# One third of the routed rows formed by GpSimd, the rest by ScalarE one behind each product

## What is computed

```python
mu = jnp.mean(xf, axis=-1, keepdims=True)
var = jnp.var(xf, axis=-1, keepdims=True)
...
tk_probs, tk_idx = jax.lax.top_k(probs, TOP_K)
...
out = _swiglu(xf, sWg, sWu, sWd)
for e in range(NUM_EXPERTS):
    out = out + w[:, e:e + 1] * _swiglu(xf, Wg[e], Wu[e], Wd[e])
return out.reshape(B, S, H)
```

## Time and profile before

| | us |
|---|---|
| median of 3 runs | 2165.62 (2164.62 to 2167.09) |
| the profiled execution | 2157.81, its span 2156.2 |
| granted TensorE clock, mean | 0.978 |
| busy: PE, DVE, ACT, POOL | 1972.2, 1245.1, 1079.3, 800.1 |
| front stage in the trace | about 1173 to 1490 |

### The profile page before, as it was taken

How to read it: one execution, slowest core, us unless ns; L and a number is a source line. 1 busy time by engine, 2 the same in 40 slices (tenths; PEclk the granted TensorE clock), 3 DMA queues, 4 the chain that set the end, 5 groups by cost and what they waited for, 6 DMA issues and landing times. The chain is left out here.

```text
span 2156.2 us, 48396 instructions
## 1 busy us (share of the span) xinstructions
PE 1972.2 (91%) x14823; PEld 1296.1 (60%) x14824; DVE 1245.1 (58%) x3875; ACT 1079.3 (50%) x2352; POOL 800.1 (37%) x1164
## 2 busy tenths in 40 slices
PE   2689999999999999999988999997999999999997
PEld 1344444454444554445545887785777777777776
DVE  5656667766667666676653954443545554545454
ACT  1245555555555555555543454452555555555553
POOL 3023323333323333233332046661444444444443
PEclk8789999999999999999989999998999999999999
DMA  7234443344443434434313355553873333333332
GB/s 239 70 93 116 120 130 117 120 116 120 136 131 111 127 109 127 131 114 132 106 63 114 110 166 207 200 185 117 221 181 58 57 53 55 55 59 55 54 55 36
DMA packets 156640, 246.08 MB, mean 114 GB/s; under 512 B 29408, under 2 KB 90592, under 8 KB 156480
## 3 DMA queue, kind: packets, MB, share of 16 engines
q1 hardware_dynamic: 120960, 189.24, 28.6%
q0 software_dynamic: 32064, 53.44, 12.0%
q10 hardware_dynamic: 3456, 1.34, 0.3%
HBM read 111.89 MB, written 90.50 MB: 94 GB/s over the span
## 5 line engine op out<-in xcount | busy, mean ns | idle before, releaser
L680 DVE CUSTOM_DVE_ANT_0 ps_rows<-ps_rows,maskrow 128x128 f32<-128x128 f32 (+1 forms) x1009 | 477.3, 514 | 295.5 <-PE ps_rows L525 287.6
L623 ACT ACTIVATE probs<-ps_cols 128x512 f32<-128x512 f32 (+3 forms) x1024 | 391.9, 435 | 391.8 <-PE ps_cols L536 385.1
L525 PE MATMUL ps_rows<-ks,qs 32*128 32x512 f32 x1984 | 406.8, 484 | 72.9 <-DVE mx L680 36.0
L532 PE MATMUL ps_cols<-qs,ks 32*128 32x512 f32 (+3 forms) x2048 | 421.9, 488 | 2.3 <-ACT probs L623 2.2
L1624 POOL DMA_INDIRECT out_dram<-y_e,to x135 | 215.5, 1596 | 348.9 <-DMA out_dram<-y_e,to 229.3
L799 POOL TENSOR_TENSOR pace<-eps 1x1 f32<-1x1 f32 x256 | 58.0, 227 | 752.6 <-ACT probs L623 752.6
L525 PEld LDWEIGHTS ps_rows<-ks,qs 32*128 32x128 f32 x1984 | 154.2, 185 | 270.0 <-DVE mx L680 223.3
L536 PE MATMUL ps_cols<-mT,ones_r 32*128 32x512 f32 (+3 forms) x1024 | 287.1, 554 | 0.0
L1753 DVE TENSOR_TENSOR h_lo<-ps_h,h_hi 128x512 fp32r<-128x512 f32 x135 | 93.4, 692 | 232.8 <-ACT h_hi L1728 232.8
L1722 ACT ACTIVATE sg_e<-ps_ge 128x512 f32<-128x512 f32 x135 | 80.8, 598 | 261.7 <-PE ps_ge L1646 261.7
L554 PE MATMUL ps_o<-probs,vt 128*32 128x512 f32 (+3 forms) x2048 | 193.7, 451 | 0.8 <-POOL probs L801 0.8
(11 more groups left out here) (218 smaller groups left out, 3852.0 us busy)
## 6 DMA issues: line engine op xcount, KB each, us to landing
xs_d<-zrows SPq DMA_DIRECT2D x45, 408.0 KB, 2.9
xr<-xs_d POOLq DMA_DIRECT2D x135, 136.0 KB
whi_d<-w_sh SPq DMA_DIRECT2D x16, 768.0 KB, 3.8
w_hi<-whi_d SPq DMA_DIRECT2D x24, 512.0 KB
xn<-in_L_attn_x_dram SPq DMA_DIRECT2D x16, 512.0 KB, 5.3
ks<-k_lin SPq DMA_DIRECT2D x64, 128.0 KB, 2.7
ks<-k_tan SPq DMA_DIRECT2D x64, 128.0 KB, 3.7
qs<-q_lin SPq DMA_DIRECT2D x64, 128.0 KB, 2.4
```

The source lines that it names most:

```text
L525: mm = nc.tensor.matmul(ps_rows[bank_of(row_no(g, it, h))][:, 0:(it + 1) * P], qs[at:at + STRIP, d.par, g, it * P:(it + 1) * P], ks[at:at ...
L532: nc.tensor.matmul(ps_cols[bank_of(col_no(n, s, e))][:, jt * P:S], ks[at:at + STRIP, b.par, gc, jt * P:(jt + 1) * P], qs[at:at + STRIP, b. ...
L623: nc.scalar.activation(probs[:, n % 2, 2 * (1 - s) + e, jt * P:S], ps_cols[bank_of(col_no(n, s, e))][:, jt * P:S], ACT.Exp).then_inc(exp_d ...
L680: nc.vector.tensor_tensor_reduce(out=bank, in0=bank, in1=maskrow[:, (TT - 1 - it) * P:S], scale=1.0, scalar=LOWEST, op0=ALU.add, op1=ALU.m ...
```

## The change

Every third tile, `own(t)`: t % 3 == 2, 21 of the 64, is formed by GpSimd itself, in its loop right before that tile's scatters, with a `tensor_scalar` (times `rstd2`, plus `nmr`) and a `tensor_copy` of `place`. They count a new semaphore, `pool_normed`. ScalarE forms the other 43, one a call: four a batch, still from batch 4 on; tile 63 stays in slot 2 of batch 14. Before each pair of scatters GpSimd waits for both counts, and SyncE does before it reloads an `xw` buffer; when it tries to is as before (six tiles a batch).

```diff
-    A_ROUND = (2, 1, 2, 1)
...
+    def own(t):
+
+        return t % 3 == 2
+
+    ACT_TILES = [t for t in range(NT) if not own(t)]
+
     def tiles_of(s, i):
 
-        n = sum(A_ROUND)
-        first = (s.off - ROWS_AT) * n + sum(A_ROUND[:i])
-        many = A_ROUND[i] if s.off < FIRST - 1 else 2
-        return range(max(first, 0), min(first + many, NT)) if s.off >= ROWS_AT else range(0)
+        at = (s.off - ROWS_AT) * IT + i
+        return ACT_TILES[at:at + 1] if s.off >= ROWS_AT else []
+
+    def formed(t):
+
+        return 2 * sum(1 for u in range(t + 1) if not own(u)), 2 * sum(1 for u in range(t + 1) if own(u))
...
             if bt >= AHEAD:
-                sp.wait_ge(normed, (bt - AHEAD + 1) * TT * 2)
+                by_act, by_pool = formed((bt - AHEAD + 1) * TT - 1)
+                sp.wait_ge(normed, by_act)
+                sp.wait_ge(pool_normed, by_pool)
...
         for t in range(NT):
             q = t % RING
-            pool.wait_ge(normed, (t + 1) * 2)
+            if own(t):
+                bt = t // TT
+                pool.wait_ge(xw_loaded[bt % AHEAD], (bt // AHEAD + 1) * 16)
+                if t >= RING:
+                    pool.wait_ge(scattered[q], t // RING * 32)
+                nc.gpsimd.tensor_scalar(row[q][:, :, 0:D], xw[:, bt % AHEAD, t % TT].unsqueeze(1).to_broadcast([P, 2, D]),
+                                        rstd2[:, t:t + 1], nmr[:, t:t + 1], ALU.mult, ALU.add).then_inc(pool_normed, 1)
+                nc.gpsimd.tensor_copy(row[q][:, :, D:D + 2], place[:, t]).then_inc(pool_normed, 1)
+            pool.wait_ge(normed, formed(t)[0])
+            pool.wait_ge(pool_normed, formed(t)[1])
```

More of the change, by code:

```diff
@@ L1255, in front_stage @@
     normed = sem("normed")
+    pool_normed = sem("pool_normed")
     scattered = [sem(f"scattered{q}") for q in range(RING)]
@@ L1303, in _ @@
                 se.load_in(sp, Batch(0, s + 2))
-            while loaded < NB and (loaded - AHEAD + 1) * TT <= (s - ROWS_AT) * sum(A_ROUND):
+            while loaded < NB and (loaded - AHEAD + 1) * TT <= (s - ROWS_AT) * 6:
                 load_rows(loaded)
@@ L1348, in norm_rows @@
                 bt, q = t // TT, t % RING
-                if t % TT == 0:
-                    act.wait_ge(xw_loaded[bt % AHEAD], (bt // AHEAD + 1) * 16)
+                act.wait_ge(xw_loaded[bt % AHEAD], (bt // AHEAD + 1) * 16)
                 if t == 0:
```

## The result

| | before | after |
|---|---|---|
| median, us | 2166.36 (2164.62 to 2167.80, 4 runs) | 2137.78 (2137.74 to 2140.31, 4 runs) |
| ratio | | 0.9873, 95% interval 0.9858 to 0.9888 |
| profiled execution, its span | 2157.81, 2156.2 | 2137.79, 2136.1 |

The change makes the kernel 28.6 us (1.3%) faster.

What follows compares the result with a forecast made beforehand. The prediction took a loop through GpSimd's scatters, not TensorE's floor, as the bound. Forming 44.0 plus usual gaps 3.0 minus filled gaps 39.0 gave +8.0 us on 2165.6, so 2174 (chance 0.38), range 2149 to 2188.

Steps and rivals of the forecast that it cites:

- What bounds the kernel: Front stage: completions visible only after GpSimd's scatter run pauses, so a GpSimd loop of 19.5 us paces, not TensorE's 17.55.
- Relief of ScalarE 0: Front stage: taking 21 us of tile forming from ScalarE gains 0, as its wait for TensorE hides that work.
- pairs 0: ScalarE's forming of tiles in pairs in slots 0 and 2 by itself costs TensorE nothing.
- SyncE 0: Before reloading xw, SyncE also waits for GpSimd's tiles: 0 unless GpSimd is a whole round behind.
- end 0: End of front stage: 23 us of TensorE's work follow tile 63 before and after, so the loop's loss carries through in full.
- A tile costs 2.2 us: GpSimd's forming: TENSOR_SCALAR 1.6, COPY 0.2, completion wait 0.25, wait with VectorE 0.15; bounds 1.1 and 2.9 us.
- Completions pass only in the forming pauses: Front-stage loop: TensorE's release falls on every second forming pause, making the round GpSimd's, 20.3 us instead of 19.5.
- Rival A: Front stage: TensorE paces at its 17.55 us floor, gaining up to 17 us, time 2150; chance 0.25.
- the ring filling up: Ring of 8 rows between ScalarE and GpSimd: GpSimd can fall 8 tiles behind, some 27 us, so cost 0.
- Collisions with VectorE, 0.15 a tile: GpSimd's forming against VectorE's hT subtraction, both reading SBUF: 0.4 us a hit, 0.4 hits a tile.
- The base of the sum: Differences read from the profiled execution of 2157.81 us were added to the median of 2165.62 us.
- Rival C: Late completions come only with recording; timed runs already sit at TensorE's floor: 0 to +8 us, 2168; chance 0.25.

Runs made afterwards that it cites:

- e2: The changed kernel, but nobody forms the 256 values of the 21 tiles, so GpSimd only scatters: 2162.25 us, ratio 0.9976 to the kernel before.
- e10: The changed kernel with GpSimd forming both tiles of every six in one place, so scatters run in twelves: 2167.15 us against 2166.14 for the kernel before.
- e17: The changed kernel with ScalarE doing the work of the 21 tiles all the same, into an unused buffer: 2139.66 us against 2159.87 for the kernel before.
- e4: The changed kernel with ScalarE forming its four tiles a round in two pairs, behind slots 0 and 2: 2137.35 us, ratio 0.986 to the kernel before.
- e13: The changed kernel with GpSimd forming each of its tiles twice, once into an unused buffer: 2151.43 us against 2158.58 for the kernel before.
- e12: The kernel before with each scatter writing 16 of the 272 columns, into a DRAM tensor of its own: 2163.27 us against 2164.73 unmodified.
- e3: The changed kernel with VectorE forming the 21 tiles and GpSimd only scattering: 2185.59 us, ratio 1.0084 to the kernel before.

## Why the prediction was wrong

**What bounds the kernel: right, with one thing missing.** TensorE's floor of 17.55, the late `ysb` and `sg` as what the rounds lose, their tie to GpSimd's scatters: after, e2 and e10 bear it out. Missing was that the kernel before itself does without them in two of nine series. No view of one profile could show that.

**Relief of ScalarE 0, pairs 0, SyncE 0, end 0: right.** e17 and e4 show the first two. SyncE waited 21.7 us in all for GpSimd's rows in after, and ScalarE, GpSimd and TensorE have no wait for its loads there. The gain of a round came through in full at the end.

**A tile costs 2.2 us: wrong, 1.42.** The TENSOR_SCALAR was taken as 1.6 from the 256-column one at 0.933 by a straight line through 0.30 at 8 columns; it took 0.77 (mean 774 ns, 757 at least). The cast of the same shape at 0.609 would have been the nearer row: the one instruction of 0.933 was a single one, straight behind a DMA. COPY took 0.18 for 0.2. The wait, put at 0.25, took about twice that: 0.78 passes between the copy's end and the next scatter, 0.48 more than usual. The Trainium skill, GPSIMD Engine Reference, "Elementwise — side-by-side cycle accounting", has 769 ns for 512 elements; the trace agrees. With 1.42 in the forecast's own sum, 20 x 1.42 + 3.0 - 39.0 = -7.6: the sign turns, but it is 2158, still 20 us too slow.

**Completions pass only in the forming pauses, and so GpSimd's round is the stage's: wrong, and the larger error.** It was read from the regular 1.58 to 1.68 us between last scatter and release. The same round held the evidence against it, in two lines of the order of time that the forecast left out:

```profile
1354.08 0.96 POOL L1389 DMA_INDIRECT xs_d<-row,pos  x1 [0.30 <-issue]
1354.78 0.69 DVE L1200 TENSOR_TENSOR ysb<-ps_y,x1s 128x512 f32<-128x512 f32 x1 [3.17 <-issue]
```

This is the first half of `ysb`, whose 24 matmuls ended about 1351.2, with the sixth scatter. It starts under the ninth, 3.5 late, but with no pause anywhere near. In all ten rounds with scatters it is so: the first half, ended between the sixth and the eighth scatter, is released 0.9 to 3.5 late while the run goes on, and only the second, ended under the ninth to the eleventh, waits for the end of the run. So completions do pass within a run, late. In after most pass in the middle of runs. Some do wait for a forming pause, 1.72 us from scatter to scatter, and come 1.2 to 1.5 behind the sixth scatter, near to what the forecast had. But they are at most 2.4 late, and TensorE doesn't stop for that. **So what failed is that TensorE's release is tied to the pauses and the round to GpSimd**; a break keeps the lateness small, and TensorE paces. Rival A had this, with 2150. e13 shows that the step fails even at the forecast's price: at 2.18 us a tile TensorE kept its floor for nine rounds with scatters. What a dear tile costs is the ring filling up, which the forecast had put at 0.

**Collisions with VectorE, 0.15 a tile: rare, and free.** Four of the 21 TENSOR_SCALARs of GpSimd in after overlap an `hT` subtraction, which has two inputs in SBUF. The most that it takes is 1.07 instead of 0.69, and GpSimd's COPY under it 0.63 instead of 0.18:

```profile
1317.80 0.76 POOL L1401 TENSOR_SCALAR row<-xw,rstd,nmr 128x512 f32<-128x512 f32 x1
1318.04 1.07 DVE L1181 TENSOR_TENSOR hT<-h,hT 128x512 fp32r<-128x512 f32 x1
...
1318.52 0.63 POOL L1403 COPY row<-place 128x4 f32<-128x4 f32 x1
```

The subtraction lost 0.38 of the 0.52 us in which both ran. The Trainium skill's rule that the forecast named (SBUF — State Buffer, "Who interferes with whom") has the second of the two blocked in full; the trace agrees with the kind of instruction and shows somewhat less. TensorE never waited for it, since its rounds are at the floor.

**The base of the sum.** Even at the floor the forecast's arithmetic gives 2148.6, 11 above the result. 4.5 of this is the stage ahead of the front, which varies from execution to execution, taken with the profiled execution of before. The rest is that the timed executions of before are 5 to 8 us over the profiled ones (2165.6 against 2157.8, 2159.9 against 2154.5) and those of after aren't (2137.8 in both). Recording doesn't make the difference: with late completions the profiled execution of e10 lies at the median (2166.94 against 2167.15), that of e12 above it. The forecast took a quick execution for the usual one; where a slow one loses the rest no profile of before shows. Rival C, which had late completions in the recording alone, falls with the timed gain of 28.6 us.

## What to carry to other kernels

Where an engine's completions are seen late while GpSimd issues indirect DMAs back to back, spread these: some work of GpSimd's own after every six was enough here, and the same work after every twelve did nothing. Time the kernel in several sessions before pricing such a stall, for it can be absent altogether. Before letting a helper engine set the pace, ask how far it may fall behind: a ring of eight tiles hid 2 us a round for nine rounds, and then it cost 6 us at once. And look at the granted clock of a round that is much longer than the rest, for TensorE's own stall can be only a part of it.

## What the runs showed of the hardware

- In an unbroken run of twelve indirect DMAs on GpSimd (0.96 us each, 0.30 apart) TensorE's completions are seen late. In the kernel before, those of matmuls that end between the sixth and the eighth come 0.9 to 3.5 us late within the run; those that end under the ninth to the eleventh come 3.7 to 6.4 late, 1.6 to 1.7 after the last. In e3, e10 and e12 some are 7 to 10 us late. 64 or 1088 bytes a row make no difference. ScalarE's signals to GpSimd pass meanwhile: scatters that waited for them follow at the same 0.30.
- With some 1.4 us of other work after every six, completions are still up to 2.4 us late (3.1 in e4 and e17), and TensorE stays at its floor.
- In the same stretches TensorE itself has gaps of 0.2 to 1.3 us between matmuls for which no wait is seen (14.7 us within `down` in e3).
- After a stretch in which PE was busy 1.65 of 3.57 us (e10), and after one of 3.97 in which it did nothing (e13), the granted clock was 0.53 and 0.54 over the next 3.6 and 3.4 us, and then 1.00 again.
- The same kernel shows neither in some series (2139 us) and both in others (2158 to 2168). What makes the difference, and by what the scatters do it, isn't settled.
- A TENSOR_SCALAR of 128x512 with two pointer operands takes 0.77 us on GpSimd and 0.55 on VectorE, so GpSimd is 1.4 times slower, not 3 times as a line through smaller shapes had it.
